# Ternary feed-forward: the squares of the inner layer in two running sums, the odd ones added by GpSimd

## The chip, the core and the metric

One core of a Trainium2 chip runs the whole program. The metric is the time of one execution in device microseconds, as the median of several runs. Engines are called by the names of the profile: TensorE (PE, its weight loads PEld), VectorE (DVE), ScalarE (ACT), GpSimd (POOL) and SyncE (SP).

## What is computed

The program is four blocks, each of cross-attention and a feed-forward, on x of 2 x 1024 tokens of 256. The change touches the third block's feed-forward alone, a ternary one:

```python
def _ternary_linear(x, w):
    alpha = jnp.mean(jnp.abs(w))
    w_t = jnp.sign(w) * (jnp.abs(w) > 0.5 * alpha).astype(w.dtype)
    ...
    rms = jnp.sqrt(jnp.sum(x * x, axis=-1, keepdims=True)) / jnp.sqrt(jnp.asarray(d, x.dtype))
    x_norm = x / (rms + EPS)
    return jnp.einsum('bsd,fd->bsf', x_norm, w_q)
h = jax.nn.gelu(_ternary_linear(x, w_up), approximate=False)
return _ternary_linear(h, w_down)
```

The inner layer h has 1024 values for each token. The second `_ternary_linear` needs the sum of the squares of those 1024 values for each token: this sum is what the change computes in another way.

## The kernel before

`align_and_ternary` (line 1009) holds the third block's attention and its ternary feed-forward. The 2048 tokens are four groups of 512 (W, line 1015), and the 1024 inner values are 8 slices f of 128 (FT). The layout is turned: a slice is 128 inner values on the partitions by 512 tokens. Every engine's order is written out by hand, and engines meet at semaphores only.

For a slice (g, f), with n = 8 g + f, the work goes this way.

- TensorE, `up(g, f)` (line 1128): four products into one of three PSUM banks. The first of a group waits for `low_part` of that group's tokens (x_lo).
- ScalarE, `hidden(g, f)` (line 1294): gelu into h (line 1299), for most slices a second gelu into hh, rounded (line 1303), and the square of h. The square of f = 0 goes straight into `total` (line 1308); the others go into one of three buffers sq (line 1313), which lie in the transposed rows xnT. A square waits until the add that read its buffer is done.
- VectorE, `split(g, f)` (line 1491): hl = h - hh (line 1501), and for the slices that ScalarE doesn't round also the cast hh (line 1497). `add_square(g, f)` (line 1504) adds sq to `total` (line 1509), for f = 1 to 7. Each add waits for the one before.
- TensorE, `squares(g)` (line 1144): four products with a column of ones turn `total` into one number for each token. It waits for the group's seventh add.
- VectorE, `root(g)` (line 1511), GpSimd, `root(g)` (line 1387, a power) and VectorE, `factors(g)` (line 1515) make the factor of each token from that number.
- TensorE, `down(g, i)` (line 1156): 16 products for 128 tokens; VectorE, `residual(g, i)` (line 1525): adds the result, times the factor, to x, and takes its statistics. `down` goes into one of a few banks and waits until the residual that read the bank is done.

Beside it run the rest of the attention (VectorE's `front`, `weigh`, `attended`; TensorE's `scores`, `values`), the first norm of the feed-forward (VectorE's `moments`, `scale_rows`; GpSimd's `spreads`, line 1381; ScalarE's `rows_x` and `high_part`; VectorE's `low_part`, line 1484), and, on GpSimd near the end, the norm of the fourth block's first 8 tiles of rows: `after.first_rows` (line 329) is a root (line 288) and 8 rows (line 301). GpSimd's order is short: four `spreads`, four `root`, and `after.first_rows` ahead of `root(3)`. VectorE's order is the long list from line 1534 on; TensorE's begins at line 1177 and ScalarE's at line 1315. A barrier of all engines ends the stage.

Of the kernel before, what the change touches and what calls it, by code (L numbers as in the profile page):

```python
# [954 lines left out]
class TernaryWeights:  # L955
# [3 lines left out]
    FT = F // P  # L959
# [49 lines left out]
def align_and_ternary(nc, ctx, K, tag, side, tw, layer, prefetch, after):  # L1009
# [5 lines left out]
    F, FT, W = tw.F, tw.FT, 512  # L1015
    NG = B * S // W
    ps = K.ps
    with ExitStack() as c:
# [10 lines left out]
        sq = [K.xnT[:, i // 2, (i % 2) * W:(i % 2 + 1) * W] for i in range(3)]  # L1029
        vec = sbuf(nc, c, tag + "vec", [P, NG, 5, 4])  # L1030
        spread = sbuf(nc, c, tag + "spread", [P, 2, 2, NT])
        total = tw.raw[0][:, 0:2 * W].rearrange("p (i w) -> p i w", i=2)
        (a_tr, a_turned, a_ps, a_used, a_mx, a_in, a_p, a_sum, a_fac, a_tp, a_tb, a_y, a_x, a_st) = semaphores(
            nc, c, tag + "a_", "tr turned ps used mx in p sum fac tp tb y x st")
        (n_vec, n_pow, n_scale, rows, x_ps, x_hi, x_lo, u_ps, h_sb, h_hi, h_lo, hh_dve, h_sq, added, q_ps, vstep, rms, v_rdy,
         y_ps, x_done) = semaphores(
            nc, c, tag, "vec pow scale rows x_ps x_hi x_lo u_ps h_sb h_hi h_lo hh_dve h_sq added q_ps vstep rms v_rdy y_ps xd")
# [19 lines left out]
        with nc.Block(no_gpsimd_drain=True) as block:  # L1057
# [7 lines left out]
            def _(pe):  # L1065
# [78 lines left out]
                def squares(g):  # L1144

                    pe.wait_ge(added, g * (FT - 1) + FT - 1)
                    if g:
                        pe.wait_ge(vstep, 3 * (g - 1) + 1)
                    else:
                        pe.wait_ge(a_tb, NG)  # L1150
                    for j in range(4):
                        m = pe.matmul(ps[:, 3, 4 * g + j:4 * g + j + 1], total[:, g % 2, j * P:(j + 1) * P], K.ones[:, 0:1],
                                      start=(j == 0), stop=(j == 3), skip_group_check=True)
                    m.then_inc(q_ps, 1)
# [112 lines left out]
            def _(act):  # L1267
# [26 lines left out]
                def hidden(g, f):  # L1294
                    n = g * FT + f
                    act.wait_ge(u_ps, n + 1)
                    if n >= 4:
                        act.wait_ge(h_lo, n - 3)
                    act.activation(h[:, n % 4, :], ps[:, n % 3, :], ACT.Gelu).then_inc(h_sb, 1)
                    if on_act(n):  # L1300
                        if g >= 2 and f == 0:
                            act.wait_ge(y_ps, 4 * (g - 1))
                        act.activation(hh[g % 2][:, f, :], ps[:, n % 3, :], ACT.Gelu).then_inc(h_hi, 1)
                    act.wait_ge(h_sb, n + 1)
                    if f == 0:
                        if g >= 2:
                            act.wait_ge(q_ps, g - 1)
                        act.activation(total[:, g % 2, :], h[:, n % 4, :], ACT.Square).then_inc(h_sq, 1)
                    else:
                        m = g * (FT - 1) + f - 1  # L1310
                        if m >= 3:
                            act.wait_ge(added, m - 2)
                        act.activation(sq[m % 3], h[:, n % 4, :], ACT.Square).then_inc(h_sq, 1)
# [89 lines left out]

            @block.vector
            def _(dve):
# [98 lines left out]
                def add_square(g, f):  # L1504
                    m = g * (FT - 1) + f - 1
                    dve.wait_ge(h_sq, g * FT + f + 1)
                    if f > 1:
                        dve.wait_ge(added, m)
                    dve.tensor_tensor(total[:, g % 2, :], total[:, g % 2, :], sq[m % 3], ALU.add).then_inc(added, 1)
# [46 lines left out]
                add_square(0, 1)  # L1556
# [6 lines left out]
                add_square(0, 3)  # L1563
# [3 lines left out]
                add_square(0, 5)  # L1567
# [10 lines left out]
                add_square(0, 7)  # L1578
# [5 lines left out]
                add_square(1, 1)  # L1584
# [7 lines left out]
                add_square(1, 3)  # L1592
# [7 lines left out]
                add_square(1, 5)  # L1600
# [4 lines left out]
                add_square(1, 7)  # L1605
                split(2, 0)
                split(2, 1)
                add_square(2, 1)
# [5 lines left out]
                add_square(2, 3)  # L1614
# [5 lines left out]
                add_square(2, 5)  # L1620
# [6 lines left out]
                add_square(2, 7)  # L1627
# [5 lines left out]
                add_square(3, 1)  # L1633
# [4 lines left out]
                add_square(3, 3)  # L1638
# [4 lines left out]
                add_square(3, 5)  # L1643
# [5 lines left out]
                add_square(3, 7)  # L1649
# [1882 lines left out]
```

## Time and profile before

| | before |
|---|---|
| median of 3 runs | 1044.92 us (1043.39 to 1045.66) |
| span of the profiled execution | 1043.2 us |
| TensorE busy | 964.7 us (92%) |
| VectorE busy | 603.3 us (58%) |
| ScalarE busy | 489.0 us (47%) |
| GpSimd busy | 287.8 us (28%) |

The span runs from the first to the last instruction of one profiled execution; that execution's own time with what lies around the span is not shown, so the span stands here beside the runs. Busy shares are means over the whole program; the touched stage is a tenth of it, and its own shares differ, which is why the rows below are taken from windows and timelines of that stage. In a timeline each row has the start and the length in microseconds, the engine, the line and the operation, what it writes and reads, how many instructions are merged in the row, and in brackets how long the engine stood idle before and what released it. A row of several instructions is as long as from the first's start to the last's end. TensorE's products overlap, so the work of a group of them is read from start to start.

### The profile page before, as it was taken

Reading aid. Unit: us, or ns where it says so; the run is one execution under the profiler, and the core shown is the slowest. Engines: PE = TensorE matmul, PEld = TensorE weight load, DVE = VectorE, ACT = ScalarE, POOL = GpSimd, SP = SyncE. Lnnn points to the kernel's source line nnn. Section 1 sums busy time; section 2 is a strip of 40 time slices with the busy share of each in tenths; the row PEclk is TensorE's granted clock in tenths of the full one; section 3 lists DMA queues with packets and bytes.
Section 4 is the critical chain, followed back from the end, with each engine's and each line's share of the span. In section 5 each row is a group of like instructions: output and inputs, shape, how many; then the busy total and the mean of one; then the engine's idle time right before and its main releaser. Section 6 shows DMA issues by size and latency. Waiting matters only on the chain. (4 is left out here: it accounts for less than half of the span.)

```text
span 1043.2 us, 18151 instructions
## 1 busy us (share of the span) xinstructions
PE 964.7 (92%) x6476; PEld 835.3 (80%) x6477; DVE 603.3 (58%) x1253; ACT 489.0 (47%) x744; POOL 287.8 (28%) x271
## 2 busy tenths in 40 slices
PE   6999999989999999877988889999998999999997
PEld 5778878878888888565777778887885799999996
DVE  5858769951223222689898999666776522222221
ACT  3654422111111111688785878255552556656561
POOL 2000000033444442280006112600000344444442
PEclk9999999999999999998999999999999999999999
DMA  9200040025667664011000010260115223322332
GB/s 295 69 1 22 21 143 21 21 77 166 181 181 210 182 168 91 15 41 41 1 1 2 1 41 2 99 231 21 41 42 171 83 45 50 48 45 48 51 45 31
DMA packets 62500, 79.38 MB, mean 76 GB/s; under 512 B 7340, under 2 KB 46855, under 8 KB 62439
## 3 DMA queue, kind: packets, MB, share of 16 engines
q1 hardware_dynamic: 48807, 59.95, 17.0%
q0 software_dynamic: 13632, 18.62, 10.2%
q8 instruction: 38, 0.62, 0.2%
q14 instruction: 23, 0.19, 0.1%
HBM read 60.73 MB, written 17.83 MB: 75 GB/s over the span
## 5 line engine op out<-in xcount | busy, mean ns | idle before, releaser
L3165 PEld LDWEIGHTS ps<-room,xn_sb 128*128 128x128 f32 x1248 | 145.6, 192 | 2.7 <-issue 0.8
L3165 PE MATMUL ps<-room,xn_sb 128*128 128x128 f32 x1248 | 146.3, 275 | 0.6 <-issue 0.6
L288 POOL TENSOR_TENSOR norm_vec<-norm_vec,powers 128x4 f32<-128x4 f32 (+2 forms) x27 | 28.9, 1071 | 360.7 <-DVE norm_vec L282 360.7
L3118 POOL DMA_INDIRECT out_x<-f_yo,f_give x39 | 62.0, 1589 | 110.5 <-DVE f_yo L3363 97.5
L3234 ACT ACTIVATE xn_sb<-w_L_ffn_w 128x1024 f32 x78 | 82.1, 1057 | 20.8 <-DVE f_te L3331 10.8
L3357 DVE TENSOR_TENSOR room<-room,ps 128x512 f32<-128x512 f32 x39 | 26.8, 687 | 109.5 <-PE ps L3165 109.5
L2857 DVE TENSOR_TENSOR room<-room,ps 128x1024 f32<-128x1024 f32 x24 | 29.3, 1219 | 104.0 <-issue 89.5
L2461 PE MATMUL ps<-b_room,room 128*128 128x256 f32 x384 | 85.6, 380 | 3.7 <-DVE room L2857 1.6
L2461 PEld LDWEIGHTS ps<-b_room,room 128*128 128x128 f32 x384 | 72.6, 190 | 14.1 <-issue 1.8
L2673 ACT ACTIVATE room<-ps 128x1024 f32<-128x1024 f32 x24 | 24.6, 1023 | 115.2 <-PE ps L2441 115.2
L2418 POOL DMA_INDIRECT acc_rows<-f_eo,f_idx x32 | 52.4, 1637 | 94.7 <-DVE f_eo L2883 50.9
L498 PE MATMUL ps<-a_vblk,a_pT 128*128 128x51 f32 (+1 forms) x640 | 74.8, 272 | 0.0
L3173 PE MATMUL ps<-w_L_ffn_w,room 128*128 x312 | 73.9, 380 | 0.9 <-DVE room L3357 0.9
L498 PEld LDWEIGHTS ps<-a_vblk,a_pT 128*128 128x128 f32 (+1 forms) x640 | 74.0, 192 | 0.2 <-issue 0.2
L744 DVE TENSOR_REDUCE a_mx<-ps 128x16 f32<-128x1232 f32 x32 | 46.0, 1436 | 28.1 <-PE ps L472 14.1
L2441 PE MATMUL ps<-f_x_room,b_room 128*128 128x256 f32 x256 | 58.7, 382 | 3.6 <-ACT f_x_room L2703 3.6
L3173 PEld LDWEIGHTS ps<-w_L_ffn_w,room 128*128 128x128 f32 x312 | 56.2, 190 | 7.1 <-issue 1.1
L3239 ACT ACTIVATE room<-ps 128x512 f32<-128x512 f32 x39 | 23.3, 597 | 77.9 <-PE ps L3165 77.1
L2452 PE MATMUL ps<-f_x_room,b_room 128*128 128x256 f32 x256 | 57.9, 379 | 0.0
L2441 PEld LDWEIGHTS ps<-f_x_room,b_room 128*128 128x128 f32 x256 | 48.0, 190 | 11.7 <-issue 3.8
L487 PE MATMUL ps<-ident,a_pr 128*128 128x128 f32 x320 | 48.0, 282 | 7.4 <-ACT a_pT L692 3.0
L2452 PEld LDWEIGHTS ps<-f_x_room,b_room 128*128 128x128 f32 x256 | 48.6, 190 | 6.6
(404 smaller groups left out, 2059.4 us busy)
## 6 DMA issues: line engine op xcount, KB each, us to landing
w_L_ffn_w<-in_L_ffn_w SPq DMA_DIRECT2D x24, 512.0 KB, 9.8
b_room<-in_L_ffn_Wg SPq DMA_DIRECT2D x16, 512.0 KB
b_room<-in_L_ffn_Wu SPq DMA_DIRECT2D x16, 512.0 KB
b_room<-in_L_ffn_Wd SPq DMA_DIRECT2D x16, 512.0 KB, 6.3
xn_rows<-xn_sb SPq DMA_DIRECT2D x8, 512.0 KB, 2.9
x_sb<-in_x SPq DMA_DIRECT2D x4, 512.0 KB, 6.4
xn_sb<-in_L_ffn_w SPq DMA_DIRECT2D x2, 1024.0 KB, 7.6
x_sb<-acc_rows SPq DMA_DIRECT2D x4, 512.0 KB, 5.9
```

What stands on the lines that cost most here:

```text
L487: m = pe.transpose(ps[0:w, 4 + r % 2, (part - lo) * P:(part - lo + 1) * P], pr[:, n % 2, part * P:part * P + w], K.ident[:, :])
L498: m = pe.matmul(ps[:, 6, h * HV:(h + 3) * HV], pT[0:w, n % 2, part, :], vblk[0:w, n // TB, part, :, :].rearrange("p j c -> p (j c)"), star ...
L744: dve.tensor_reduce(mxt, sc, AX.X, ALU.max).then_inc(sh_step, 1)
L2418: pool.indirect_dma_start(acc_dram[:, :], bass.IndirectOffsetOnAxis(ap=idx[:, n:n + 1], axis=0), eo[e % 2][:, b, :], None, compute_op=ALU. ...
L2441: m = pe.matmul(ps[:, f // 2, (f % 2) * W:(f % 2 + 1) * W], g[:, k, f * P:(f + 1) * P], rhs[k], start=(k == 0), stop=(k == KT - 1))
L2452: m = pe.matmul(ps[:, 2 + f // 2, (f % 2) * W:(f % 2 + 1) * W], u[:, k, f * P:(f + 1) * P], rhs[k], start=(k == 0), stop=(k == KT - 1))
L2461: m = pe.matmul(ps[:, 4 + p, j * D:(j + 1) * D], hT[p][:, f, j * P:(j + 1) * P], w[:, f, :], start=(f == 0), stop=(f == FT - 1))
L2857: dve.tensor_tensor(hT[p][:, :, :].rearrange("p a c -> p (a c)"), ge[p][:, :], ps[:, 2:4, :].rearrange("p a c -> p (a c)"), ALU.mult).then ...
L3118: pool.indirect_dma_start(out_rows[:, :], bass.IndirectOffsetOnAxis(ap=give[:, j:j + 1], axis=0), yo[j % 2][:, :], None, compute_op=ALU.ad ...
L3165: m = pe.matmul(ps[:, banks[p], f * P:(f + 1) * P], wb[p][:, n, i, f * P:(f + 1) * P], xsT[p][:, i * P:(i + 1) * P], start=(i == 0), stop= ...
L3173: m = pe.matmul(ps[:, Y_BANK, 0:D], hid[p][:, f * P:(f + 1) * P], w2[:, e, f, :], start=(f == 0), stop=(f == FT - 1))
L3234: act.activation(wb[p][:, n, :, :], w[:, e, :, :], ACT.Copy).then_inc(w_sb, 1)
```

## The change

There are now two running sums for each group. `total` takes the even slices and a new buffer `odd_total` the odd ones. ScalarE writes the squares of f = 0 and f = 1 straight into them and the other six into one of four buffers (three before). VectorE adds f = 2, 4, 6 to `total`, three adds a group instead of seven. GpSimd adds f = 3, 5, 7 to `odd_total`, with a semaphore of its own, `odd_added`. `squares(g)` waits for both and makes eight products with ones instead of four, all into the same numbers. GpSimd's order changes: the adds stand between the other work, `spreads(3)` now comes ahead of `root(0)`, and the 8 rows of the next norm are taken in pairs with adds between them and `root(3)` ahead of the last pair.

```diff
-        sq = [K.xnT[:, i // 2, (i % 2) * W:(i % 2 + 1) * W] for i in range(3)]
+        sq = [K.xnT[:, i // 2, (i % 2) * W:(i % 2 + 1) * W] for i in range(4)]
...
+        odd_total = sbuf(nc, c, tag + "odd_total", [P, 2, W])
...
                 def squares(g):
-                    pe.wait_ge(added, g * (FT - 1) + FT - 1)
+                    pe.wait_ge(added, 3 * g + 3)
+                    pe.wait_ge(odd_added, 3 * g + 3)
...
-                    for j in range(4):
-                        m = pe.matmul(ps[:, 3, 4 * g + j:4 * g + j + 1], total[:, g % 2, j * P:(j + 1) * P], K.ones[:, 0:1],
-                                      start=(j == 0), stop=(j == 3), skip_group_check=True)
+                    for odd, part in enumerate((total, odd_total)):
+                        for j in range(4):
+                            m = pe.matmul(ps[:, 3, 4 * g + j:4 * g + j + 1], part[:, g % 2, j * P:(j + 1) * P], K.ones[:, 0:1],
+                                          start=(j == 0 and not odd), stop=(j == 3 and odd == 1), skip_group_check=True)
...
-                    if f == 0:
+                    if f < 2:
...
-                        act.activation(total[:, g % 2, :], h[:, n % 4, :], ACT.Square).then_inc(h_sq, 1)
+                        act.activation((total, odd_total)[f][:, g % 2, :], h[:, n % 4, :], ACT.Square).then_inc(h_sq, 1)
                     else:
-                        m = g * (FT - 1) + f - 1
-                        if m >= 3:
-                            act.wait_ge(added, m - 2)
-                        act.activation(sq[m % 3], h[:, n % 4, :], ACT.Square).then_inc(h_sq, 1)
+                        m = g * (FT - 2) + f - 2
+                        if m >= 4:
+                            act.wait_ge((added, odd_added)[m % 2], m // 2 - 1)
+                        act.activation(sq[m % 4], h[:, n % 4, :], ACT.Square).then_inc(h_sq, 1)
...
+                def add_odd(g, f):
+                    m = g * (FT - 2) + f - 2
+                    pool.wait_ge(h_sq, g * FT + f + 1)
+                    if f > 3:
+                        pool.wait_ge(odd_added, m // 2)
+                    pool.tensor_tensor(odd_total[:, g % 2, :], odd_total[:, g % 2, :], sq[m % 4], ALU.add).then_inc(odd_added, 1)
...
                 spreads(0)
                 spreads(1)
+                add_odd(0, 3)
+                add_odd(0, 5)
                 spreads(2)
+                add_odd(0, 7)
+                spreads(3)
                 root(0)
-                spreads(3)
+                add_odd(1, 3)
+                add_odd(1, 5)
+                add_odd(1, 7)
+                add_odd(2, 3)
                 root(1)
+                add_odd(2, 5)
+                add_odd(2, 7)
                 root(2)
-                after.first_rows(pool)
+                after.norm.root(pool, 0)
+                add_odd(3, 3)
+                pool.wait_ge(after.norm.s_pow, 1)
+                after.norm.on_pool(pool, 0, 2, after.rows)
+                add_odd(3, 5)
+                after.norm.on_pool(pool, 2, 4, after.rows)
+                add_odd(3, 7)
+                after.norm.on_pool(pool, 4, 6, after.rows)
                 root(3)
+                after.norm.on_pool(pool, 6, TB, after.rows)
```

VectorE's `add_square` counts and waits accordingly, and its calls for f = 1, 3, 5, 7 are taken out of the list of all four groups; nothing else in that list moves.

## Rows read from the trace of the kernel before

**Rows 1.** Windows: length, PE, PEld, DVE, ACT, POOL busy, clock, DMA, GB/s.
```profile
595.00:605.00 10.00, 6.90 (x31) 5.42 (x29) 9.76 (x27) 9.20 (x16) 1.54 (x1) 0.90 0.00 1
625.00:635.00 10.00, 10.00 (x61) 8.41 (x60) 8.78 (x17) 8.87 (x18) 0.00 (x0) 1.00 0.01 2
```

**Rows 2.** Windows of 2 us around TensorE's longest wait.
```profile
600.00:602.00 2.00, 0.00 (x0) 0.00 (x0) 1.97 (x6) 1.99 (x4) 0.00 (x0) 1.00 0.00 0
602.00:604.00 2.00, 1.52 (x4) 1.20 (x5) 1.86 (x11) 1.53 (x3) 0.54 (x1) 0.73 0.00 0
604.00:606.00 2.00, 2.00 (x6) 1.63 (x5) 1.93 (x5) 1.66 (x4) 1.26 (x1) 0.50 0.16 31
606.00:608.00 2.00, 2.00 (x11) 1.65 (x11) 1.93 (x5) 1.99 (x4) 0.00 (x0) 0.92 0.96 304
```

**Rows 3.** TensorE's timeline: the last scores, and the three waits for VectorE.
```profile
588.16 2.01 PE L946 MATMUL ps<-keys_a,xnT_sb 128*128 128x77 f32 x16 [0.71 <-ACT xnT_sb L1270]
...
602.48 0.50 PE L1140 MATMUL ps<-f_xh,tu 128*128 128x512 f32 x1 [3.10 <-DVE f_xl L1487]
...
611.43 0.36 PE L1173 MATMUL ps<-f_td,f_hh 128*128 128x256 f32 x1 [0.28 <-DVE x_sb L1438]
...
620.46 0.39 PE L1173 MATMUL ps<-f_td,f_hh 128*128 128x256 f32 x1 [0.46 <-DVE x_sb L1529]
```

**Rows 4.** TensorE's timeline at the products with ones of groups 0, 2 and 3.
```profile
613.85 0.95 PE L1152 MATMUL ps<-ones,room 128*128 128x1 f32 x8
614.66 0.64 PE L1069 MATMUL ps<-ident,xn_sb 128*128 128x128 f32 x4
...
644.62 1.05 PE L1152 MATMUL ps<-ones,room 128*128 128x1 f32 x8
...
660.18 0.99 PE L1152 MATMUL ps<-ones,room 128*128 128x1 f32 x8
661.03 0.37 PE L1173 MATMUL ps<-f_td,f_hh 128*128 128x256 f32 x1
```

**Rows 5.** VectorE's timeline: front(3), the cast of split(0, 5), low_part(2) and (3), attended(3, 0).
```profile
590.29 0.47 DVE L1411 TENSOR_TENSOR f_sm<-ps,keys_c 128x308 f32<-128x308 f32 x1
...
596.35 0.42 DVE L1497 CAST f_hh<-f_h 128x512 fp32r<-128x512 f32 x1
...
601.15 1.27 DVE L1487 TENSOR_TENSOR f_xl<-ps,f_xh 128x512 fp32r<-128x512 f32 x2
...
610.42 0.48 DVE L1438 SCALAR_TENSOR_TENSOR x_sb<-ps,f_av,x_sb 128x256 f32<-128x256 f32 x1
```

**Rows 6.** ScalarE's timeline: gelu of slice (0, 5), square of slice (2, 7).
```profile
595.51 0.58 ACT L1299 ACTIVATE f_h<-ps 128x512 f32<-128x512 f32 x1
...
642.56 0.63 ACT L1313 ACTIVATE xnT_sb<-f_h 128x512 f32<-128x512 f32 x1
```

**Rows 7.** Groups by line and shape: VectorE's adds, GpSimd's adds elsewhere; busy us, mean ns.
```profile
L1509 DVE TENSOR_TENSOR room<-room,xnT_sb 128x512 f32<-128x512 f32 x28 | 19.2, 687 | 0.1
...
L2392 POOL TENSOR_TENSOR f_eo<-f_eo,x_sb 128x512 f32<-128x512 f32 x6 | 7.6, 1269 | 39.6 <-ACT f_eo L2683 39.5
```

**Rows 8.** GpSimd's timeline: the next norm's root and two of its eight rows.
```profile
649.15 2.01 POOL L288 TENSOR_TENSOR norm_vec<-norm_vec,powers 128x8 f32<-128x8 f32 x1 [1.35 <-DVE norm_vec L282]
...
653.55 2.42 POOL L301 TENSOR_SCALAR xn_sb<-x_sb,norm_vec 128x256 f32<-128x256 f32 x1
...
662.58 1.21 POOL L301 TENSOR_SCALAR xn_sb<-x_sb,norm_vec 128x256 f32<-128x256 f32 x1
```

**Rows 9.** VectorE's timeline: beside GpSimd's rows, and the end of the stage.
```profile
653.75 0.69 DVE L1501 TENSOR_TENSOR f_hl<-f_h,f_hh 128x512 fp32r<-128x512 f32 x1
...
654.95 0.89 DVE L1501 TENSOR_TENSOR f_hl<-f_h,f_hh 128x512 fp32r<-128x512 f32 x1
...
664.83 0.17 DVE L1518 TENSOR_SCALAR f_vec<-f_vec 128x4 f32<-128x4 f32 x1 [3.00 <-POOL f_vec L1389]
...
668.57 0.43 DVE L1532 BATCH_NORM_STATS2 bn_st<-x_sb 128x6 f32<-128x256 f32 x1
```

More of the change, by code:

```diff
@@ L1032, in align_and_ternary @@
         total = tw.raw[0][:, 0:2 * W].rearrange("p (i w) -> p i w", i=2)
+        odd_total = sbuf(nc, c, tag + "odd_total", [P, 2, W])
         (a_tr, a_turned, a_ps, a_used, a_mx, a_in, a_p, a_sum, a_fac, a_tp, a_tb, a_y, a_x, a_st) = semaphores(
             nc, c, tag + "a_", "tr turned ps used mx in p sum fac tp tb y x st")
-        (n_vec, n_pow, n_scale, rows, x_ps, x_hi, x_lo, u_ps, h_sb, h_hi, h_lo, hh_dve, h_sq, added, q_ps, vstep, rms, v_rdy,
+        (n_vec, n_pow, n_scale, rows, x_ps, x_hi, x_lo, u_ps, h_sb, h_hi, h_lo, hh_dve, h_sq, added, odd_added, q_ps, vstep, rms, v_rdy,
          y_ps, x_done) = semaphores(
-            nc, c, tag, "vec pow scale rows x_ps x_hi x_lo u_ps h_sb h_hi h_lo hh_dve h_sq added q_ps vstep rms v_rdy y_ps xd")
+            nc, c, tag, "vec pow scale rows x_ps x_hi x_lo u_ps h_sb h_hi h_lo hh_dve h_sq added odd_added q_ps vstep rms v_rdy y_ps xd")
         gate_a = K.gate[:, 0, layer:layer + 1]
@@ L1504, in add_square @@
                 def add_square(g, f):
-                    m = g * (FT - 1) + f - 1
+                    m = g * (FT - 2) + f - 2
                     dve.wait_ge(h_sq, g * FT + f + 1)
-                    if f > 1:
-                        dve.wait_ge(added, m)
-                    dve.tensor_tensor(total[:, g % 2, :], total[:, g % 2, :], sq[m % 3], ALU.add).then_inc(added, 1)
+                    if f > 2:
+                        dve.wait_ge(added, m // 2)
+                    dve.tensor_tensor(total[:, g % 2, :], total[:, g % 2, :], sq[m % 4], ALU.add).then_inc(added, 1)
                 def root(g):
@@ L1555, in _ @@
                 split(0, 1)
-                add_square(0, 1)
                 split(0, 2)
@@ L1562, in _ @@
                 split(0, 3)
-                add_square(0, 3)
                 split(0, 4)
@@ L1566, in _ @@
                 split(0, 5)
-                add_square(0, 5)
                 attended(2, 0)
@@ L1577, in _ @@
                 split(0, 7)
-                add_square(0, 7)
                 split(1, 0)
@@ L1583, in _ @@
                 attended(3, 1)
-                add_square(1, 1)
                 moments(3)
@@ L1591, in _ @@
                 low_part(5)
-                add_square(1, 3)
                 factors(0)
@@ L1599, in _ @@
                 scale_rows(3)
-                add_square(1, 5)
                 split(1, 6)
@@ L1604, in _ @@
                 split(1, 7)
-                add_square(1, 7)
                 split(2, 0)
                 split(2, 1)
-                add_square(2, 1)
                 residual(0, 3)
@@ L1613, in _ @@
                 low_part(6)
-                add_square(2, 3)
                 split(2, 4)
@@ L1619, in _ @@
                 low_part(7)
-                add_square(2, 5)
                 split(2, 6)
@@ L1626, in _ @@
                 split(2, 7)
-                add_square(2, 7)
                 residual(1, 2)
@@ L1632, in _ @@
                 split(3, 1)
-                add_square(3, 1)
                 after.first_moments(dve)
@@ L1637, in _ @@
                 split(3, 3)
-                add_square(3, 3)
                 split(3, 4)
@@ L1642, in _ @@
                 split(3, 5)
-                add_square(3, 5)
                 split(3, 6)
@@ L1648, in _ @@
                 residual(2, 1)
-                add_square(3, 7)
                 residual(2, 2)
```

## The prediction

> **What bounds the kernel now.** I first split the stretch that the change touches into windows, then read TensorE's timeline for its waits, then the timelines of VectorE, ScalarE and GpSimd at those waits. The ternary feed-forward runs from about 563 to 669 us of the span. The windows show two regimes [rows 1]. Near 595 to 605 us VectorE is full (9.76 of 10 us) and TensorE is not (6.90). From 625 to 635 us TensorE is full (10.00), with VectorE beside it at 8.78. So an instruction taken from VectorE pays in the first regime, and an instruction added to TensorE costs in the second.
>
> TensorE's waits say the same. From 602 to 661 us it waits three times, for 3.10, 0.28 and 0.46 us, each time for VectorE [rows 3]. The 3.10 us are the wait of `up(1, 0)` for `low_part(3)`. In it TensorE's granted clock falls: 1.00 while it stands still at 600 to 602 us, then 0.73, 0.50 (1.2 instead of 2.4 GHz) and 0.92 [rows 2]. After that TensorE follows itself until the end, where VectorE stands 3.00 us for GpSimd's root and starts its last statistics at 668.57 us [rows 9].
>
> **The change part by part.** All shifts are of the end of this stage; what follows it starts behind a barrier of all engines and moves as a whole.
>
> *VectorE loses 16 of 28 adds.* One is 687 ns long [rows 7], and starts follow each other at 0.60 us (653.75 to 654.95 us is two instructions) [rows 9]; 16 x 0.60 = 9.6 us. Only what lies ahead of a wait of TensorE counts, so I follow the order of VectorE up to each. Ahead of `low_part(3)` three adds go (f = 1, 3, 5 of group 0). The first buys nothing: `front(3)`, at 590.29 us [rows 5], reads scores whose products run from 588.16 for 2.01 us [rows 3], to 590.17 us. The two others buy 1.2 us, but `split(0, 5)` begins with a cast, at 596.35 us [rows 5], of a tile that ScalarE writes from 595.51 for 0.58 us [rows 6]; it can start no sooner than some 596.15 us, so VectorE waits 0.4 us. That leaves 0.8 us: `low_part(2)` and `low_part(3)`, which now start at 601.15 us [rows 5], come at 600.35, and `up(1, 0)` at about 601.7 instead of 602.48 us. Then `add_square(0, 7)` goes, and `attended(3, 0)`, now at 610.42 us [rows 5], comes 0.8 + 0.6 = 1.4 us earlier. `down(0, 0)` (611.43 us, with 0.28 us of wait [rows 3]) waits for exactly that. **-1.4 us.** Whether the clock still falls in the shorter wait doesn't enter: between the two points TensorE's work fits either way, and VectorE sets the time. Two further adds, (1, 1) and (1, 3), go ahead of the residual for which `down(0, 2)` waits 0.46 us [rows 3]; the residual then comes well before that product. **-0.5 us.** The other ten adds lie where TensorE is full and VectorE would only wait longer for it: nothing.
>
> *TensorE gets 16 more products with ones.* Each group now has two sums to turn. Four products of float32 are 8 records, and from their first to the next work TensorE takes 0.81 us (613.85 to 614.66) and 0.85 us (660.18 to 661.03) [rows 4]. Four groups at 0.85 us: **+3.4 us** (3.2 to 3.7). No wait covers them: the first group's come after `down(0, 0)`, and all four lie where TensorE follows itself. This is the largest term, and it is why I don't pass the 9.6 us on to the result.
>
> *GpSimd gets 12 adds.* The same form, two 128x512 float32 inputs in SBUF, takes 1269 ns on GpSimd elsewhere in this kernel [rows 7]: 15.2 us if it runs alone. It does not. A row of the layer norm takes 1.21 us on GpSimd when VectorE is not at two SBUF inputs and 2.42 us when VectorE runs nothing else [rows 8]; VectorE's instruction then takes 0.69, once 0.89 us [rows 9]. So I bound an add at 1.27 and 2.5 us and take 1.7, since in the new order VectorE's two-input work is 8 subtractions and 3 adds of 0.60 us a group, 6.6 of the 15.6 us from one group's products to the next (644.62 to 660.18 [rows 4]); at half speed for that share an add takes 1.6. Eight adds are early enough: (2, 3), (2, 5) and those of groups 0 and 1 end microseconds before their products, and `root(0)`, now behind `spreads(3)`, still ends before VectorE has done `split(1, 3)` and `low_part(5)`. Two places are tight.
>
> The first is `squares(2)`. The square of (2, 7) is written from 642.56 for 0.63 us [rows 6] and `squares(2)` follows at 644.62 us [rows 4], 1.43 us after. An add of 1.27 to 1.9 us with its two semaphores takes 1.4 to 2.0: **+0.2 us** (0 to 0.6).
>
> The second is `squares(3)`. GpSimd now has, between the root of the next norm (649.15, 2.01 us [rows 8]) and `squares(3)`, three adds and four rows. With 2.01 us for the root, 1.7 for each of the first two adds, about 1.8 and 1.6 for the first two rows (half speed beside VectorE), 1.21 for the next two and 1.27 for the last add, it is done 12.5 us after the root begins; the root begins where it does now, give or take 0.3 us, since VectorE has lost an add ahead of it but waits longer for `squares(2)`. That is 661.4 to 661.9 us. TensorE, 0.9 us later than now by the terms so far (-1.4 - 0.5 + 3 x 0.85 + 0.2), arrives at 661.1 instead of 660.18 us. **+0.6 us** (0 to 2.5). ScalarE's squares wait for the add two places earlier on the same engine; (3, 7), the last, needs the add of (3, 3), done 3.7 us after that root begins, near 653 us, while (3, 7) is among the last products of its group, so ScalarE is not held up.
>
> *The tail.* VectorE's last four residuals now start only after GpSimd's root, which stands behind eight rows, and the last one trails TensorE by one residual more than it must: `factors(3)` resumes at 664.83 us, and the last of the four residuals' statistics start at 668.57 us [rows 9]. In the new order the root comes before the last two rows, VectorE catches up while the last three `down` run, and only one residual is left behind TensorE. **-0.9 us.** The two rows that then follow end before TensorE does.
>
> *The sum:* -1.4 - 0.5 + 3.4 + 0.2 + 0.6 - 0.9 = **+1.4 us**. The profiled span of 1043.2 us would become 1044.6. What lies around the span is not shown for that execution; the median of the runs is 1.7 us above the span, and I add the shift to the median: 1044.92 + 1.4 = **1046.3 us**. With every term at its better end it is -1.4 - 0.5 + 3.2 + 0 + 0 - 0.9 = +0.4; at its worse end, with the first gain lost, 0 - 0.5 + 3.7 + 0.6 + 2.5 - 0.9 = +5.4.
>
> **The rivals.** *GpSimd's adds take VectorE's time (slower).* A two-input add may keep VectorE's two-input instructions from starting for as long as it runs, 1.27 us. Against it: beside the layer norm's rows VectorE lost at most 0.2 us (0.89 against 0.69 [rows 9]). For it: those rows have one input, and the one form with two was not seen beside such work. Place: the adds of (0, 5) and (0, 7), which fall on `split(0, 5)` and on `add_square(0, 6)`; if each delays VectorE by 0.6 us the 1.4 us shrink to 0.2. The last add then also meets a waiting GpSimd: about 1 us more at `squares(3)`. 1.4 + 1.2 + 1.0 = +3.6: 1048.5 us. It decides from about 1.9 us an add, or 0.9 us a subtraction. The Trainium skill states this in SBUF — State Buffer, section "SBUF: two separate sides": the shared pair of ports is an exclusive lock, held for the whole instruction by whichever starts first, and the other side fully blocks. The trace agrees only in part: GpSimd's row doubles, but VectorE's instructions keep their length, which a lock held by GpSimd for a whole row would not allow.
>
> *The relief reaches further (no change or faster).* If the clock stays at 2.4 GHz through 602 to 606 us, TensorE saves 1.7 us there (2 us each at 0.27, 0.50 and 0.08 under full [rows 2]), and if VectorE and ScalarE keep up, that arrives at the end; with no stall at `squares(3)` the sum is 1.4 - 1.7 - 0.6 = -0.9: 1044.0 us. For a gain over 0.2% (about 2.1 us, what a measurement of this kernel can tell from no change) the extra products would have to hide as well, and TensorE's full windows speak against that.
>
> *VectorE's adds were cover only (slower).* If the 1.4 us are eaten by ScalarE, which is at 9.20 of 10 us at 595 to 605 us [rows 1], the products stay: 1.4 + 1.4 = +2.8, 1047.7 us.
>
> **How the numbers follow.** The sum within its terms (+0.4 to +2.1 us): 0.46. Relief reaching further, down to no change: 0.14; beyond -2.1 us: 0.08. GpSimd's adds taking VectorE's time: 0.22, and gains eaten or terms at their worse ends: 0.10. So faster by over 0.2% is 0.08, within 0.2% is 0.46 + 0.14 = 0.60, slower is 0.32. The range leaves out the gain beyond -1.1 us (0.10) and what lies beyond +3.9 us (0.08): 1043.8 to 1048.8 us.
>
> **What would show it.** Right: the wait of `up(1, 0)` falls from 3.10 to about 2.3 us; `down(0, 0)` starts near 610.0 us; each group's products are 16 records of about 1.7 us; `squares(3)` starts near 661.6 us, behind GpSimd; the last statistics start some 1.4 us later than 668.57 us. Wrong: a GpSimd add with a mean over 2 us or VectorE's subtractions over 0.75 us (the first rival); a clock that never falls near 603 us with TensorE ahead by over 2 us at `down(0, 0)` (relief); `squares` that cost TensorE less than 0.6 us more a group, which would break the largest term.

## The result, and the profile after

The changed kernel takes 1048.36 us (median of 20 runs, 1045.73 to 1051.79), the kernel before 1045.13 us on the same chip (20 runs, 1042.1 to 1048.77). The ratio is 1.0032 with a 95% interval of 1.0021 to 1.0044: the change costs 3.2 us. The forecast was 1046.3 us, "within 0.2%" the likeliest. The range held the time, but the sum was 2 us short, and the case that came is the first rival's sign and nearly its size. The range held because it left room for that rival (a chance of 0.22), not because the sum was right.

Three executions of the changed kernel were profiled, this one and two more among the experiments. Here is the page of the first (engine, busy us, share, instructions), and three groups between 585 and 676 us: VectorE's subtractions, VectorE's adds, GpSimd's adds (busy us, mean ns | idle time before them).

```profile
span 1049.3 us, 18200 instructions
...
L1528 DVE TENSOR_TENSOR f_hl<-f_h,f_hh 128x512 fp32r<-128x512 f32 x32 | 24.4, 783 | 3.0 <-ACT f_hh L1306 2.5
...
L1536 DVE TENSOR_TENSOR room<-room,xnT_sb 128x512 f32<-128x512 f32 x12 | 8.7, 723 | 0.1
...
L1399 POOL TENSOR_TENSOR f_odd_total<-f_odd_total,xnT_sb 128x512 f32<-128x512 f32 x12 | 16.7, 1395 | 25.0 <-ACT xnT_sb L1316 25.0
```

VectorE has 12 adds where it had 28 [rows 7], but each is now 723 instead of 687 ns. GpSimd's add is 1395 ns long where the prediction took 1.7 us. It named a subtraction above 0.75 us as the sign of the first rival, and the subtractions stand at 783 ns. The windows that answer to [rows 1] (of the third profile, `e11_changed`, whose stage starts 0.5 us later in the span than before's) show the same two regimes. TensorE is full in the second, and there VectorE is relieved (6.82 us busy where it had 8.78); in the first it hardly is (9.46 where it had 9.76):

```profile
595.00:605.00 10.00, 7.09 (x30) 5.66 (x31) 9.46 (x26) 9.67 (x17) 3.01 (x2) 0.88 0.00 0
625.00:635.00 10.00, 10.00 (x65) 8.54 (x63) 6.82 (x16) 7.74 (x16) 0.00 (x0) 1.00 0.01 2
```

What becomes late is seen on TensorE's timeline of the first profile, where the stage starts 2.45 us later in the span than before (565.80 against 563.35 us). First the wait of `up(1, 0)` and that of `down(0, 0)`, then the products with ones of group 0 and of group 3 (the two answer to [rows 3] and [rows 4]):

```profile
605.04 0.50 PE L1141 MATMUL ps<-f_xh,tu 128*128 128x512 f32 x1 [2.06 <-DVE f_xl L1514]
...
613.93 0.36 PE L1176 MATMUL ps<-f_td,f_hh 128*128 128x256 f32 x1 [0.56 <-DVE x_sb L1465]
...
616.35 0.95 PE L1155 MATMUL ps<-ones,room 128*128 128x1 f32 x8
617.16 1.03 PE L1155 MATMUL ps<-ones,f_odd_total 128*128 128x1 f32 x8
618.05 0.63 PE L1070 MATMUL ps<-ident,xn_sb 128*128 128x128 f32 x4
...
665.83 1.02 PE L1155 MATMUL ps<-ones,room 128*128 128x1 f32 x8 [0.95 <-issue]
666.71 1.03 PE L1155 MATMUL ps<-ones,f_odd_total 128*128 128x1 f32 x8
667.61 0.36 PE L1176 MATMUL ps<-f_td,f_hh 128*128 128x256 f32 x1
```

Two things are read here. From the first product with ones to the next work TensorE now takes 1.70 us (616.35 to 618.05) and 1.78 us (665.83 to 667.61), twice what it took [rows 4]: 16 records a group, as forecast. And ahead of group 3's products TensorE stands still. "Issue" names no engine, but GpSimd's last add ends just then. It is the last of these four (the second one is used further down):

```profile
591.80 1.26 POOL L1399 TENSOR_TENSOR f_odd_total<-f_odd_total,xnT_sb 128x512 f32<-128x512 f32 x1 [0.62 <-ACT xnT_sb L1316]
...
646.84 1.42 POOL L1399 TENSOR_TENSOR f_odd_total<-f_odd_total,xnT_sb 128x512 f32<-128x512 f32 x1 [3.60 <-ACT xnT_sb L1316]
...
660.18 1.47 POOL L1399 TENSOR_TENSOR f_odd_total<-f_odd_total,xnT_sb 128x512 f32<-128x512 f32 x1
...
664.46 1.26 POOL L1399 TENSOR_TENSOR f_odd_total<-f_odd_total,xnT_sb 128x512 f32<-128x512 f32 x1
```

664.46 + 1.26 is 665.72 us, and the product starts at 665.83. In this execution something more follows. The windows behind that wait (columns as in [rows 1]; the seventh is the granted clock):

```profile
666.00:668.00 2.00, 2.00 (x19) 2.00 (x19) 0.16 (x1) 0.00 (x0) 2.00 (x2) 1.00 0.03 8
668.00:670.00 2.00, 2.00 (x15) 2.00 (x14) 0.73 (x4) 0.00 (x0) 1.99 (x3) 0.72 0.00 0
670.00:672.00 2.00, 2.00 (x11) 2.00 (x11) 1.57 (x4) 0.00 (x0) 1.55 (x2) 0.50 0.00 0
672.00:674.00 2.00, 2.00 (x18) 2.00 (x17) 0.76 (x2) 0.00 (x0) 0.00 (x0) 0.93 0.00 0
```

The clock goes to half (0.50, 1.2 instead of 2.4 GHz) while TensorE is full with the last `down`. That is a second reason why this execution is long, and whether it belongs to the change had to be tried.

To compare executions, whose parts outside the stage also differ by a microsecond or two, all that follows is counted from the stage's first product on TensorE (563.35 us in the profile of before) to the first product of the next stage (676.46 us in this one, 669.39 before). "Wait" is the time from the start of TensorE's last product before `squares(3)` to the start of its first, 0.12 where there is none. One execution each of "adds on VectorE" (1665.63 us) and "root first" (1425.48 us) stands far outside the others and is not in the ratios.

| | stage | `down(0, 0)` | `squares(2)` | `squares(3)` | wait | subtraction, mean | falls of the clock | ratio, 95% |
|---|---|---|---|---|---|---|---|---|
| before | 106.04 | 48.09 | 81.28 | 96.84 | 0.12 | 698 ns | 39.6 | |
| changed, first | 110.65 | 48.13 | 82.55 | 100.02 | 1.23 | 783 | 0.7, 28.0, 103.1 | 1.0021 to 1.0044 |
| changed, second | 111.68 | 47.62 | 82.02 | 99.49 | 1.23 | 782 | 39.2, 100.7 | 1.0017 to 1.0063 |
| changed, third | 108.70 | 47.65 | 82.06 | 99.54 | 1.24 | 783 | 1.2, 38.7 | 1.0017 to 1.0045 |
| add of one column | 105.90 | 46.73 | 80.82 | 96.84 | 0.12 | 696 | 39.2 | 0.9977 to 1.0004 |
| four products | 106.43 | 47.68 | 80.82 | 98.18 | 1.23 | 853 | 39.4 | 0.9994 to 1.0019 |
| adds on VectorE | 107.79 | 48.32 | 82.63 | 98.73 | 0.12 | 707 | 1.0, 38.6 | 0.9999 to 1.0029 |
| root first | 105.10 | 48.12 | 81.32 | 96.88 | 0.12 | 698 | 39.6 | 0.9972 to 0.9992 |
| joined | 109.30 | 48.23 | 82.46 | 101.01 | 1.32 | 818 | 39.5, 83.9 | 1.0037 to 1.0063 |
| one input | 107.25 | 47.03 | 81.58 | 98.09 | 0.54 | 692 | 0.4, 27.7 | 1.0015 to 1.0035 |
| filled, first | 108.73 | 47.64 | 82.08 | 99.66 | 0.11 | 767 | 1.2, 38.7 | 1.0027 to 1.0058 |
| filled, second | 108.71 | 47.66 | 82.08 | 99.55 | 0.33 | 783 | 39.3 | 1.0014 to 1.0037 |
| postponed | 105.82 | 46.81 | 82.04 | 97.60 | 0.12 | 698 | 39.4 | 0.997 to 1.0001 |

The third profile is the one for the sums: its clock falls are those of before, but for one at the very start. In it the stage is 2.66 us longer than before. The profiled executions of the changed kernel took 1051.01 (first) and 1046.07 us (third), near the two ends of the result's 20 runs; the median lies between them. How well a stage repeats shows where nothing was changed: up to `squares(3)` "root first" follows before within 0.04 us, and up to `squares(2)` the second and third profile of the changed kernel and both filled ones agree within 0.05 us.

### The profile page after: what moved, and what is told of

Read it like the earlier page. It is cut to its first block and busy times, and to the rows that moved or that the text cites. A ratio compares the mean times of both kernels' runs of the same rounds, so it can differ in the third digit from the quotient of the medians.

```text
span 1049.3 us, 18200 instructions
## 1 busy us (share of the span) xinstructions
PE 974.2 (93%) x6508; PEld 843.8 (80%) x6509; DVE 600.8 (57%) x1237; ACT 489.0 (47%) x744; POOL 303.3 (29%) x283
```

## The experiments

**The adds cut to one column.** The first question was whether the products or GpSimd's adds make it slow. Here the adds keep their places, waits and semaphores, and lose nearly all of their work.

```
-pool.tensor_tensor(odd_total[:, g % 2, :], odd_total[:, g % 2, :], sq[m % 4], ALU.add)
+pool.tensor_tensor(odd_total[:, g % 2, 0:1], odd_total[:, g % 2, 0:1], sq[m % 4][:, 0:1], ALU.add)
```

> The changed kernel, with GpSimd's twelve adds cut to one column of 512 (the odd sums of the other 511 tokens are left out); order, waits and the eight products stay. Stage length, from TensorE's first product of the stage to its first of the next: 106.0 us before, 110.7 us changed. Theory 1 (a two-input add of GpSimd keeps VectorE's two-input instructions from starting while it runs, and that takes VectorE's gain and starts the stalls): VectorE's subtractions fall back to 0.69 us each, attended(3, 0) comes 1.4 us earlier against the stage's start, no wait at squares(2) and squares(3): stage 106.5 to 107.5 us, time 0 to 0.15% over before. Theory 2 (the extra products are the whole loss, GpSimd's adds run beside VectorE): only the waits at squares(2) and (3), about 1 us, go: 109 to 110 us.

The stage took 105.90 us, 0.14 less than before, and the ratio is 0.999. `down(0, 0)` came 1.36 us earlier than before, which is the prediction's 1.4, there is no wait at `squares(3)`, and the subtractions are as short as before. At `down(0, 0)` no wait is left either: VectorE's `attended(3, 0)` is 1.49 us earlier (45.58 against 47.07 us of the stage), and TensorE, at half clock from 39.2 us on, comes last. The groups, as above:

```profile
L1528 DVE TENSOR_TENSOR f_hl<-f_h,f_hh 128x512 fp32r<-128x512 f32 x32 | 21.9, 696 | 5.2 <-ACT f_hh L1306 4.8
...
L1399 POOL TENSOR_TENSOR f_odd_total<-f_odd_total,xnT_sb 128x1 f32<-128x1 f32 x12 | 4.2, 347 | 29.6 <-ACT xnT_sb L1316 29.5
```

So the bodies of 12 adds on GpSimd cost the stage 2.80 us (108.70 against 105.90), with 16 more products in both. VectorE's order is the same in both, so where it loses the time can be read instruction by instruction. VectorE beside the first and the third add in the third profile of the changed kernel (start, duration):

```profile
589.93 1.19 DVE L1507 TENSOR_TENSOR f_spread<-norm_vec,f_spread 128x4 f32<-128x4 f32 x1
591.15 0.16 DVE L1509 SCALAR_TENSOR_TENSOR f_spread<-norm_vec,f_spread 128x4 f32<-128x4 f32 x1
...
605.92 0.77 DVE L1455 TENSOR_SCALAR f_av<-f_av,gates 128x4 f32<-128x4 f32 x1
```

GpSimd in the same profile:

```profile
589.84 1.26 POOL L1399 TENSOR_TENSOR f_odd_total<-f_odd_total,xnT_sb 128x512 f32<-128x512 f32 x1 [0.61 <-ACT xnT_sb L1316]
...
605.38 1.29 POOL L1399 TENSOR_TENSOR f_odd_total<-f_odd_total,xnT_sb 128x512 f32<-128x512 f32 x1
```

And the same two VectorE instructions with the adds cut to one column:

```profile
588.81 0.16 DVE L1507 TENSOR_TENSOR f_spread<-norm_vec,f_spread 128x4 f32<-128x4 f32 x1
...
604.30 0.23 DVE L1455 TENSOR_SCALAR f_av<-f_av,gates 128x4 f32<-128x4 f32 x1
```

An instruction over four columns takes 1.19 instead of 0.16 us and ends at 591.12, just where the add does (591.10); the other takes 0.77 instead of 0.23 and ends at 606.69, the add at 606.67. VectorE begins and then stands until GpSimd's add is through. That is 1.03 + 0.54 us. With one column VectorE waits 0.43 us for TensorE's scores behind the first of them, which covers a part, and `down(0, 0)` is 0.92 us later than with one column.

**The odd sums left out of the products.** The other half alone: the adds stay whole, `squares` waits for both sums as in the changed kernel, and turns only one.

```
-for odd, part in enumerate((total, odd_total)):
-    for j in range(4):
-        m = pe.matmul(..., part[:, g % 2, j * P:(j + 1) * P], ...)
+for j in range(4):
+    m = pe.matmul(..., total[:, g % 2, j * P:(j + 1) * P], ...)
```

> The changed kernel with four products with ones a group instead of eight: the odd sums are still made and waited for, but left out of the result. The products' 16 records fall to 8, 1.70 to 1.78 us a group to 0.81 to 0.92, 3.5 us in four groups. Theory 1 (GpSimd's adds hold VectorE): attended(3, 0) and down(0, 0) stay where they are in the changed kernel against the stage's start, and the stage ends at 110.7 - 3.5 = 107.2 us or, since TensorE then waits longer for the last add of GpSimd, up to 108.5 us: still slower than before by 0.1 to 0.25%. Theory 2 (products are the whole loss): as fast as before or faster, 104 to 106 us.

The stage took 106.43 us, 2.27 less than the third profile, though four groups' products are 3.6 us shorter by their own rows. `down(0, 0)` and the wait at `squares(3)` are the same to 0.03 us. The missing 1.3 us are mostly waits that the third profile doesn't have, 0.83 and 0.14 us. The larger stands at 659.81 us; here are TensorE, then VectorE, then GpSimd, of this kernel:

```profile
659.81 0.35 PE L1175 MATMUL ps<-f_td,f_hh 128*128 128x256 f32 x1 [0.83 <-DVE x_sb L1555]
...
657.61 1.66 DVE L1527 TENSOR_TENSOR f_hl<-f_h,f_hh 128x512 fp32r<-128x512 f32 x1
659.19 0.47 DVE L1555 SCALAR_TENSOR_TENSOR x_sb<-ps,f_vec,x_sb 128x256 f32<-128x256 f32 x1
...
657.26 1.45 POOL L1398 TENSOR_TENSOR f_odd_total<-f_odd_total,xnT_sb 128x512 f32<-128x512 f32 x1
```

A subtraction starts 0.35 us after GpSimd's add, takes 1.66 us instead of some 0.69, and TensorE waits. So the two costs of the change overlap: what the products cost depends on what VectorE is late with.

**The adds on VectorE.** Two sums and 16 products a group as in the changed kernel, but all adds on VectorE, in the places where before had them.

```
-pool.tensor_tensor(odd_total[:, g % 2, :], ...)   # add_odd(g, f), in GpSimd's list
+dve.tensor_tensor(odd_total[:, g % 2, :], ...)    # in VectorE's, where add_square(g, 3), (g, 5), (g, 7) stood
...
```

> The changed kernel with the twelve odd adds on VectorE, in the places where before had them; two sums, eight products and GpSimd's new order of the rest stay. VectorE has 24 adds (28 before). Theory 1: no instruction of VectorE is held; the stage is before's 106.0 + 3.5 for the products - 0.9 for the earlier root(3) - 0.5 for the add (1, 1) that is gone: 107.5 to 108.5 us, faster than the changed kernel by 0.2%. Theory 2: VectorE has lost GpSimd's help: 110.7 us or more.

The stage took 107.79 us, 0.91 less than with GpSimd's help, although VectorE has 12 more adds to do. `down(0, 0)` is 0.67 us later than in the changed kernel, `squares(3)` 0.81 us earlier, without a wait. The help is worth less than it costs. The timed ratio (1.0014, up to 1.0029) doesn't separate it from the changed kernel's, so this ranking is the profiles'.

**The root alone.** The edit at the end of GpSimd's list, on the kernel before:

```
-after.first_rows(pool)
-root(3)
+after.norm.root(pool, 0)
+pool.wait_ge(after.norm.s_pow, 1)
+after.norm.on_pool(pool, 0, 6, after.rows)
+root(3)
+after.norm.on_pool(pool, 6, TB, after.rows)
```

> The kernel before with one part of the change alone: GpSimd's root(3) ahead of the last two of the next norm's eight rows. Both theories, as the prediction's term for the tail: VectorE's wait of 3.00 us for root(3) falls to about 1 us, only one residual is left when TensorE ends, the stage is 0.9 us shorter, 105.1 us; the time 0.1% under before, within what a measurement can tell from none. If the rows that now come later delay the next stage's first turns, its first products wait and nothing is gained.

The stage took 105.10 us, 0.94 less, and the ratio is 0.9982 (0.9972 to 0.9992). The tail's term holds by itself, and this kernel is faster than both. VectorE resumes after 1.15 us of wait for GpSimd where it stood 3.00 us [rows 9]:

```profile
664.50 0.17 DVE L1521 TENSOR_SCALAR f_vec<-f_vec 128x4 f32<-128x4 f32 x1 [1.15 <-POOL f_vec L1389]
```

**One sum joined by VectorE.** If the products are the larger cost, one add a group on VectorE could replace them: GpSimd keeps the odd sum, VectorE adds it to the even one, four products remain.

```
+def join(g):
+    dve.wait_ge(added, 4 * g + 3)
+    dve.wait_ge(odd_added, 3 * g + 3)
+    dve.tensor_tensor(total[:, g % 2, :], total[:, g % 2, :], odd_total[:, g % 2, :], ALU.add).then_inc(added, 1)
...
```

> GpSimd's odd sums as in the changed kernel, but VectorE adds the odd sum to the even one (one add a group, in the place of the add of f = 7), and TensorE keeps four products a group. Takes away the 3.5 us of products and keeps GpSimd's adds. Theory 1 (GpSimd's two-input adds hold VectorE): about the 106.4 us of the run with four products, plus up to 0.6 us at squares(2) and squares(3) for the join behind GpSimd's last add: 106.4 to 107.6 us, not faster than before. Rival (with the products away the relief of VectorE, 12 adds fewer than before, shows): 103 to 105 us and 0.1 to 0.3% under before.

It missed by 1.7 us or more: 109.30 us, and the slowest of all by the ratio (1.005). VectorE, in order, now waits for GpSimd, and TensorE for VectorE. VectorE's last join, and TensorE at the products of group 2:

```profile
664.62 0.97 DVE L1540 TENSOR_TENSOR room<-room,f_odd_total 128x512 f32<-128x512 f32 x1 [0.99 <-POOL f_odd_total L1398]
...
647.10 1.05 PE L1153 MATMUL ps<-ones,room 128*128 128x1 f32 x8 [1.20 <-DVE room L1540]
```

Behind the wait at 647.10 us the clock fell once more (at 83.9 us of the stage, for 3.4 us).

**One input.** Does GpSimd hold VectorE by being busy so long, or by the form of its instruction? The add is replaced by an instruction with one tensor input and about the same duration; the odd sums are left out.

```
-pool.tensor_tensor(odd_total[:, g % 2, :], odd_total[:, g % 2, :], sq[m % 4], ALU.add)
+pool.tensor_scalar(odd_total[:, g % 2, 0:256], sq[m % 4][:, 0:256], K.npow[:, 0:1], K.hpow[:, 0:1], ALU.subtract, ALU.mult)
```

> The changed kernel with each of GpSimd's twelve adds replaced by an instruction of the same length (about 1.21 us, as the norm's rows) that reads one SBUF tensor of 256 columns and writes 256 (the odd sums are left out); order, waits and the eight products stay. Theory 1a (it takes GpSimd's two inputs, or its 512 columns, to hold VectorE): VectorE's subtractions stay near 0.70 us on the mean and 0.9 at most, the stage is like that of the one-column run, 105.9, plus up to 1 us for the last waits: 106 to 107 us. Theory 1b (any instruction of GpSimd that reads SBUF holds VectorE's two-input instructions for as long as it runs): subtractions of 1.3 to 1.8 us, stage 109 to 110.7 us as in the changed kernel.

```profile
L1529 DVE TENSOR_TENSOR f_hl<-f_h,f_hh 128x512 fp32r<-128x512 f32 x32 | 21.7, 692 | 5.0 <-ACT f_hh L1306 4.5
...
L1399 POOL TENSOR_SCALAR f_odd_total<-xnT_sb,powers 128x256 f32<-128x256 f32 x12 | 17.1, 1421 | 24.4 <-ACT xnT_sb L1316 24.4
```

GpSimd is as busy as with the adds (1421 against 1395 ns), and VectorE's subtractions are as short as before (692 ns, the longest 0.77 us). So it isn't the time that GpSimd is busy: its add with two inputs of 512 columns holds VectorE's subtractions, an equally long instruction with one input of 256 doesn't. Operation, inputs and columns changed together here, and no run took them apart. The number of inputs alone doesn't decide it. GpSimd's power in `spreads` has two, of eight columns, and two subtractions beside it kept their length (GpSimd, then VectorE, in the third profile of the changed kernel):

```profile
587.22 2.01 POOL L1388 TENSOR_TENSOR f_spread<-f_spread,powers 128x8 f32<-128x8 f32 x1 [11.81 <-DVE f_spread L1493]
...
588.11 1.29 DVE L1528 TENSOR_TENSOR f_hl<-f_h,f_hh 128x512 fp32r<-128x512 f32 x2
```

The layer norm's rows [rows 8] have one input of 256 columns, which is why VectorE's subtractions lost at most 0.2 us beside them [rows 9]. Beside such an instruction not all of VectorE is free: a `TENSOR_SCALAR` over four columns took 0.43 instead of 0.23 us in this kernel and ended with GpSimd's instruction (616.27 beside 616.24 us).

The stage took 107.25 us: 1.45 less than with the adds, 1.35 more than with one column. Of the 1.35 us, 0.4 each stand at `squares(2)` and `squares(3)`, where TensorE waits for GpSimd (from product to product 0.62 against 0.23 us and 0.54 against 0.12). Another 0.3 us stand ahead of `down(0, 0)`, where this execution's clock fell at 27.7 instead of 39.2 us; whether that fall makes them was not tried. So about half of the adds' 2.80 us is VectorE held up, and of the other half some 0.8 us is GpSimd's busy time itself. The timed ratio of this kernel is 1.0025, 2.6 us, where its profiled stage explains 1.2. This execution was the shortest of its ten and ran at a mean clock of 0.986, the nine others at 0.980 to 0.983; what lowered theirs was not seen.

**The wait filled.** Is the clock's fall behind `squares(3)` the work of the wait? TensorE gets four products without use in it.

```
 down(3, 0)
+pe.wait_ge(h_sb, 31)
+pe.wait_ge(h_hi, rounded_by_act(31))
+unread(pe, K, 0, 4)
 squares(3)
```

> The changed kernel with four idle products of TensorE ahead of squares(3) (eight records, about 1.0 us, results not read), in the 1.1 us in which it waits for GpSimd's last add. If it is that wait, followed by 1.8 us of products with one column, after which the clock falls: the granted clock stays at 2.4 GHz in the last downs, 48 records take 5.9 instead of 7.4 us, the stage is 1.0 to 1.5 us shorter (109.2 to 109.7). If the fall belongs to something else it stays, and the stage is 110.7 us or up to 0.3 more.

108.73 us, with no fall behind `squares(3)` and the rest as in the changed kernel; but the ratio, 1.0043, is no better than the changed kernel's. So both kernels were run again, and the changed one once more beside the filled one.

> The changed kernel once more, on the chip of these runs, for the spread from execution to execution: stage 110.7 us with a fall of the clock near 28 and near 103 us after the stage's start in each profile if these falls follow from its order of work (both theories); falls in other places or none if they are chance, and then up to 1.7 us of the loss in the first profile was chance with each.

> The changed kernel with idle products ahead of squares(3), in more rounds and beside the changed kernel, since its profile was 2 to 3 us shorter than the changed kernel's while its median was not. If the fall of the clock at the end costs the executions what it costs the profiles, the ratio to before is 1.0015 to 1.002 below the changed kernel's; if the fall belongs to single executions, the two ratios agree within 0.1%.

> The changed kernel, for the comparison with the filled one on the same chip: ratio to before 1.003 to 1.004, stage 110.7 to 111.7 us by both readings, with a fall of the clock behind squares(3).

In the second profile of the changed kernel the clock fell at the same place and for longer, 6.8 us (windows as above):

```profile
662.00:664.00 2.00, 2.00 (x15) 2.00 (x16) 0.00 (x0) 0.00 (x0) 2.00 (x2) 0.77 0.04 8
664.00:666.00 2.00, 2.00 (x10) 2.00 (x11) 0.42 (x3) 0.00 (x0) 1.55 (x3) 0.50 0.00 0
666.00:668.00 2.00, 2.00 (x12) 2.00 (x11) 1.23 (x4) 0.00 (x0) 2.00 (x2) 0.50 0.00 0
```

In the third it didn't fall at all, with the same wait ahead of it (663.39 us, beside 1.23 and 1.24 in the table):

```profile
666.00:668.00 2.00, 2.00 (x19) 2.00 (x18) 1.13 (x5) 0.00 (x0) 2.00 (x3) 1.00 0.00 0
```

From `squares(3)` to the next stage it is 10.63 and 12.19 us with the fall (first and second profile) and 9.16 without it, so the fall makes 1.5 and 3.0 us. The first profile's stage has 0.5 us more ahead of `squares(3)`. The fall came in two of three executions with the wait, in none of two with the wait filled. But the ratios of filled and unfilled kernel overlap throughout (1.0043 and 1.0026 against 1.0040 and 1.0031): what the fall costs an ordinary execution is not settled.

The mean granted clock of every execution says a little more. The changed kernel's 41 executions had 0.983 in the mean, the filled kernel's 19 the same, and the 91 of before that ran beside the experiments 0.985. At 0.986 the changed kernel took 1046.3 us (mean of 7) and before 1045.2 us (36); at 0.981 it took 1051.2 us (11) and before 1047.3 us (4). So the changed kernel runs more often at a lower clock, filling this one wait doesn't undo that, and a part of the 3.2 us goes with it. How large that part is, and where the falls lie in executions without a profile, is open. The sums below go by the third profile, whose stage is 2.66 us longer without the fall.

**The adds put off.** If the early adds on VectorE delay `attended(3, 0)`, they can also be done later, by VectorE itself. On the kernel with the root first, eight buffers of squares instead of three let the adds (0, 4) to (0, 7) follow `attended(3, 1)` and (1, 1) to (1, 3) follow `residual(0, 1)`; `squares(0)` follows `down(0, 1)`.

```
-act.wait_ge(added, m - 2)     # sq[m % 3]
+act.wait_ge(added, m - 7)     # sq[m % 8]
...
```

> The kernel before with the earlier root(3), and VectorE relieved by order instead of by GpSimd: eight buffers for squares, VectorE's adds (0, 4) to (0, 7) put off until after attended(3, 1) and (1, 1) to (1, 3) until after residual(0, 1), squares(0) one down later. No GpSimd add, four products a group. If what counts is VectorE's work ahead of low_part(3), attended(3, 0) and residual(0, 0) (the prediction's reading of TensorE's waits), attended(3, 0) comes 1.2 to 1.5 us earlier than 47.1 us after the stage's start, the stage is 1.0 to 1.8 us shorter than the 105.1 of the run with the earlier root alone, 103.3 to 104.1, and the time 0.25 to 0.35% under before. If the work put off is given back (TensorE waiting for residual(0, 0) or at squares(0)), the stage is 105 us and the time 0.15 to 0.2% under before.

`attended(3, 0)` came 1.84 us earlier in the stage than before (45.23 against 47.07) and `down(0, 0)` 1.28. The stage took 105.82 us, 0.72 more than without the edit. The gain is given back at the next two waits of TensorE, for a residual that the adds now delay (1.01 us where 0.46 stood with the earlier root alone) and for a subtraction behind it (1.14 us where there was no wait):

```profile
620.99 0.39 PE L1173 MATMUL ps<-f_td,f_hh 128*128 128x256 f32 x1 [1.01 <-DVE x_sb L1532]
...
631.08 0.39 PE L1173 MATMUL ps<-f_td,f_hh 128*128 128x256 f32 x1 [1.14 <-DVE f_hl L1504]
```

## Why the prediction was right or wrong

Its steps against the third profile of the changed kernel, counted within the stage:

| step | forecast | measured | how |
|---|---|---|---|
| adds gone ahead of `down(0, 0)` | -1.4 | -0.44 | 47.65 against 48.09 |
| wait of `down(0, 2)` | -0.5 | -0.6 | 0.23 against 0.85 |
| products with ones | +3.4 | +3.6 | 1.71 + 1.70 + 1.78 + 1.78 against 0.81 + 0.81 + 0.91 + 0.85 |
| `squares(2)` behind GpSimd | +0.2 | +0.15 | 0.49 against 0.34 |
| `squares(3)` behind GpSimd | +0.6 | +1.1 | 1.24 against 0.12 |
| the tail | -0.9 | -0.97 | from `squares(3)`'s end: 7.38 against 8.35 |
| in none of these steps | | -0.2 | what is left |
| sum | +1.4 | +2.66 | 108.70 against 106.04 |

The three waits are measured from the start of TensorE's product ahead of the wait to the start of the one behind it, so the step of `down(0, 2)` is a little larger than the 0.46 us of idle time in [rows 3]. No run says what the -0.2 us left over are.

*The step that failed is the first.* Its mechanism was right: with the adds emptied the gain is 1.36 us. Its size was wrong because the work was taken off VectorE but its time was not: two of GpSimd's adds, (0, 3) and (0, 7), fall on small VectorE instructions with nothing to spare and hold them to the adds' end. The rival had put the loss at 1.2 of the 1.4 us; it was 0.96. It had named the adds of (0, 5) and (0, 7) and the instructions `split(0, 5)` and `add_square(0, 6)`. In the third profile the add of (0, 5) runs from 597.78 us beside attended rows, which read PSUM and kept their length (0.87 us for two), and it was the neighbours of (0, 3) and (0, 7) that were held.

*The second is the size of the wait at `squares(3)`.* GpSimd's chain from the next norm's root to the last add was put at 12.5 us and took 12.95 (650.34 to 663.29 us), and its root began 0.69 us later in the stage than before, where the prediction allowed 0.3. TensorE in turn arrived 0.7 us later than assumed, for the most part by the first step, and so the wait is 0.5 us longer and the start 1.2 us later than forecast.

*What let both pass* was the reading of the trace of before. "VectorE's instructions keep their length" is right for [rows 8] and [rows 9], but those rows of GpSimd have one input, and the change brings a form with two. The prediction said so, and still gave the rival 0.22. The Trainium skill, SBUF — State Buffer, section "SBUF: two separate sides", states an exclusive lock for a whole instruction, between a VectorE instruction with two SBUF inputs and a GpSimd instruction that reads SBUF. The runs agree for the two-input add of 512 columns (1.19 us for an instruction of 0.16, 1.67 for a subtraction of 0.69), and not for the one-input instruction (subtractions of 692 ns) nor for the power of eight columns (two subtractions in 1.29 us). VectorE's timeline of the first profile has two such subtractions; the adds at 646.84 and 660.18 us above run beside them:

```profile
647.14 1.67 DVE L1528 TENSOR_TENSOR f_hl<-f_h,f_hh 128x512 fp32r<-128x512 f32 x1
...
660.52 1.67 DVE L1528 TENSOR_TENSOR f_hl<-f_h,f_hh 128x512 fp32r<-128x512 f32 x1
```

*What held.* The largest term, the products, to 0.2 us; the tail to 0.1 us, also alone. The chip bears out that most of VectorE's 16 adds were cover: gone from its queue and with nothing in their place, they gave 1.36 us, and the whole change 0.14.

*The other rivals.* "Relief reaches further" didn't come: the clock still fell near 39 us of the stage in the second and third profile. In the first it fell at 28.0 instead, and `up(1, 0)` ran at full speed; from `up(1, 0)` to `down(0, 0)` it took 8.89 us (605.04 to 613.93), in the third, at half speed, 8.89 too (38.76 to 47.65). In the changed kernel TensorE's clock does not set that point, as the prediction had it; with the adds of one column no wait for VectorE is left there, and TensorE's own work sets it. One reading of the prediction was off without bearing on its sum: in before the clock does not fall in the wait of `up(1, 0)` but 0.4 us behind it (39.6 against 39.13 us of the stage). "VectorE's adds were cover only" is refuted by the kernel with one column, where ScalarE didn't eat the 1.4 us.

## What to carry to other kernels

Before an elementwise operation goes to an idle GpSimd, price it in VectorE's time: find a row of the same form on GpSimd (operation, inputs from SBUF and columns) with VectorE's work beside it, and count as held, up to the end of that row, the instructions of VectorE that can fall beside it and read SBUF alone: the two-input ones, and small `TENSOR_SCALAR`s too. A row with another form doesn't answer the question. And when a change is a bundle, run its parts alone: here the one edit of order at the end of GpSimd's queue was worth 1 us by itself, and the two others cost more than that.

## What the runs showed of the hardware

A two-input add of 128x512 float32 on GpSimd, 1.26 us at its shortest, held VectorE's instructions until it ended. Small ones ended with it (0.16 became 1.19 us); a subtraction of 0.69 us became 1.67 and ended 0.55 us behind it (648.81 against 648.26 us in the first profile). A `TENSOR_SCALAR` over four columns with a second small operand was held (0.23 to 0.77 us), and so was one with a single input, 0.16 us long in before. Here it is in the third profile of the changed kernel, VectorE, then GpSimd, ending at 619.16 and 619.13 us:

```profile
618.24 0.92 DVE L1545 TENSOR_SCALAR f_vec<-f_vec 128x4 f32<-128x4 f32 x1
...
617.84 1.29 POOL L1399 TENSOR_TENSOR f_odd_total<-f_odd_total,xnT_sb 128x512 f32<-128x512 f32 x1
```

Two instructions of VectorE that read PSUM beside such an add kept their length (0.87 us for both, as without one). A one-input GpSimd instruction of 1.42 us in the mean held none of the subtractions, and neither did a two-input power of 2.01 us over eight columns.

The granted clock fell in some executions of one kernel and not in others at the same place, behind the same wait: for 3.4 us, for 6.8 us, and not at all.
